# First stage of a hybrid block: attention units of one query block for two heads, with scores of 64 rows in row halves of TensorE

## The reference

```
x = X                                             # 16 x 512 tokens x 256
x = x + attn_a(layernorm(x))                      # 16 heads of 64, exact GELU on the heads, inner residual
x = x + ffn(layernorm(x))                         # ternary weights 256 -> 1024 -> 256, relu
x = x + attn_b(layernorm(x))                      # 16 heads of 16, rope, biases
x = x + ffn(layernorm(x))                         # the same ffn again
attn_a(X):  Q, K, V = X@Wq, X@Wk, X@Wv            # 256 -> 1024 each
            A = softmax(Q (K/8)^T) V ;  P = gelu(A) @ Wpost ;  return X + P
ffn(x):     Wq = clip(round(W / (mean|W| + 1e-5)), -1, 1) ;  relu(x@Wq1^T + b1) @ Wq2^T + b2
```

## Time and profile before

| | us |
|---|---|
| median of three runs | 4102.15 (4093.28 to 4102.24) |
| the profiled execution | 4105.4 |
| its span, first to last instruction | 4103.6 |
| PE, DVE, ACT, POOL busy | 3809.1, 2602.2, 2378.6, 1928.0 |
| first and last start of a score matmul of the first stage | 29.1, 2330.4 |

### The profile page before, as it was taken

How to read it: one execution, slowest core, us unless ns; L and a number is a source line. 1 busy time by engine, 2 the same in 40 slices (tenths; PEclk the granted TensorE clock), 3 DMA queues, 4 the chain that set the end, 5 groups by cost and what they waited for, 6 DMA issues and landing times.

```text
span 4103.6 us, 65459 instructions
## 1 busy us (share of the span) xinstructions
PE 3809.1 (93%) x23682; PEld 2700.6 (66%) x23682; DVE 2602.2 (63%) x4147; ACT 2378.6 (58%) x4593; POOL 1928.0 (47%) x1219
## 2 busy tenths in 40 slices
PE   7999999999999999999999878999999999999987
PEld 5777777777777777777777654555555555555544
DVE  5666666566566666656666756666666666666662
ACT  4655655556565555656556435666666666666654
POOL 3454555445455554545545444444444444444412
PEclk9999999999999999999999979999999999999998
DMA  4443443434434433443443423222222222222220
GB/s 128 93 103 88 93 101 92 97 91 98 101 84 97 103 89 92 103 94 87 103 98 83 112 53 52 53 53 53 53 53 53 53 53 53 53 53 53 48 43 16
DMA packets 152368, 315.59 MB, mean 77 GB/s; under 512 B 23088, under 2 KB 76720, under 8 KB 152048
## 3 DMA queue, kind: packets, MB, share of 16 engines
q1 hardware_dynamic: 152048, 311.39, 35.3%
HBM read 33.43 MB, written 25.17 MB: 14 GB/s over the span
## 4 chain that ended last, share of the span: by engine, by line
PE 56%; DVE 21%; ACT 13%; issue 7%; POOL 3%; SPq 1%; DMA 0%; DVEq 0%; POOLq 0%; ACTq 0%
PE ps_o L624 10%; DVE neg_max L970 7%; ACT e_a L788 6%; PE ps_o L701 5%; PE ps_t L216 5%; DVE max_b L1111 4%; PE ps_t L737 4%; PE ps_s L674 3%; ACT raw_a L812 3%; PE ps_t L660 3%; PE ps_t L223 3%; PE ps_t L728 3%; PE ps_t L608 3%; PE ps_m L216 2%; DVE xn L1089 2%
## 5 line engine op out<-in xcount | busy, mean ns | idle before, releaser
L497 POOL TENSOR_TENSOR e_a<-e_a,recip 128x1024 f32<-128x1024 f32 x512 | 969.5, 1893 | 1050.2 <-DVE recip L977 1050.2
L788 ACT ACTIVATE e_a<-ps_s,neg_max 128x512 f32<-128x512 f32 x1024 | 694.0, 684 | 245.4 <-DVE neg_max L970 234.2
L828 ACT ACTIVATE et<-ps_s 128x1024 f32<-128x1024 f32 x512 | 523.5, 1023 | 434.9 <-PE ps_s L688 434.9
L1111 DVE TENSOR_REDUCE max_b<-ps_s 128x2 f32<-128x1024 f32 x512 | 623.8, 1219 | 210.4 <-PE ps_s L674 209.1
L970 DVE TENSOR_REDUCE neg_max<-ps_s 128x2 f32<-128x1024 f32 x512 | 621.0, 1213 | 19.2 <-PE ps_s L596 19.2
L624 PE MATMUL ps_o<-et_a,v_a 128*64 128x256 f32 x4096 | 470.3, 382 | 0.0
L608 PE MATMUL ps_t<-ident,e_a 128*128 128x128 f32 x2736 | 394.6, 275 | 42.0 <-DVE et_a L984 35.8
L595 PE MATMUL ps_s<-stack_a 128*128 128x512 f32 x1024 | 412.5, 403 | 9.2 <-ACT e_a L788 7.7
L531 POOL TENSOR_TENSOR h_lo<-h,h_hi 128x512 fp32r<-128x512 f32 x256 | 329.3, 1302 | 180.9 <-ACT h_hi L872 180.9
L596 PE MATMUL ps_s<-stack_a 128*128 128x512 f32 x1024 | 402.1, 393 | 0.0
L608 PEld LDWEIGHTS ps_t<-ident,e_a 128*128 128x128 f32 x2736 | 321.1, 141 | 110.8 <-DVE et_a L984 51.9
(11 more groups left out here) (207 smaller groups left out, 7976.9 us busy)
## 6 DMA issues: line engine op xcount, KB each, us to landing
stack_a<-raw_a SPq DMA_DIRECT2D x256, 384.0 KB, 4.7
stack_a<-raw_a SPq DMA_DIRECT2D x256, 256.0 KB, 4.3
stack_a<-raw_a SPq DMA_DIRECT2D x256, 128.0 KB, 3.5
q_stack<-roped_q SPq DMA_DIRECT2D x256, 64.0 KB
k_stack<-roped_k SPq DMA_DIRECT2D x256, 64.0 KB
x_a<-X SPq DMA_DIRECT2D x16, 512.0 KB, 3.6
X<-x_a SPq DMA_DIRECT2D x16, 512.0 KB, 2.9
x_ahead<-X SPq DMA_DIRECT2D x16, 512.0 KB, 3.9
```

Of the source, the lines that this page charges most:

```text
L497: nc.gpsimd.tensor_tensor(e_a[:, u % 4, :, :], e_a[:, u % 4, :, :], factor, ALU.mult).then_inc(e_normed, 1)
L788: ins = nc.scalar.activation(e_a[:, u % 4, j, :], ps_s[:, 2 * (u % 2) + j, :], ACT.Exp, bias=neg_max[:, u % 4, j:j + 1], accum_out=sums[:, ...
L828: nc.scalar.activation(et[:, v % 5, :, :], ps_s[:, 2:4, :], ACT.Exp)\
L1111: nc.vector.reduce_max(max_b[:, u // 4 % 2, :, u % 4], ps_s[:, score_bank(u):score_bank(u) + 2, :], AX.X, negate=True).then_inc(max_done, 1)
```

## The change

A unit becomes one query block for both heads of a pair; four units are still a pair. The six DMAs a pair and `stack_a` are gone. The scores of a head are three matmuls of 64 rows, directly from `raw_a`: head 0 from rows 0 to 63, head 1 from rows 64 to 127, alternating, into different banks. One call makes two units, in even slots only, 12 matmuls, and it waits for the exponentials of every earlier unit. The lead of the scores over the transposes is four slots in place of three; exponentials have five buffers in place of four. The values of a pair are made in two halves, each of 8 products, in odd slots, ahead of the slot's transposes. The table is laid out so that nearly every slot has one product; the output projection fills a bank for each of four token blocks, in place of two blocks a fill. In slots 4 and 20 of a batch element, VectorE copies both fills of the transposes. W1 and W2 are loaded in slot 40, their sums are taken in slots 471 and 473, and quantising is in slots 504 and 506. At the start, ScalarE makes the high parts of four of the six weight pieces.

```diff
-        XT, QK_FIRST, VALUE_SLOTS = -10, -8, ((-6, -5, -2, -1), (3, 3, 7, 15))
-        POST = ((27, 31), (42, 43))
+        XT, QK_SLOTS = -9, (-7, -6)
+        FIRST_VALUES, VALUE_SLOTS = (-5, -4, -1, 0), ((-8, -5, -4, -1), (7, 8, 15, 16))
+        POST, LAST_POSTS = ((32, 32, 35, 36), (43, 44, 51, 52)), (45, 46, 47, 48)
...
+        GELUS, BOTH_TURNED = (19, 35), (4, 20)
+        LEAD = 4
+        LOAD_W, LOAD_WB, LOAD_REST, SPLIT, ABS = 40, 484, 503, (508, 509), (471, 473)
+        GAMMA, QUANTISE, SCALE, CLEAR = 474, (504, 506), 514, (513, 514)
...
-                    for h in range(2):
-                        src = slice(HA * h, HA * (h + 1))
-                        dst = stack_a[:, n % 2, h, :, :].bitcast(F32)
-                        sp.dma_start(dst[0:HA, 0, :], raw[src, 0, :]).then_inc(stacked[n % 2], 16)
-                        sp.dma_start(dst[0:HA, 1:3, :], raw[src, 2:4, :]).then_inc(stacked[n % 2], 16)
-                        sp.dma_start(dst[HA:P, :, :], raw[src, 1:4, :]).then_inc(stacked[n % 2], 16)
...
                 def a_scores(u):
-                    if u >= 2:
-                        pe.wait_ge(a_exp_done, u - 1)
-                    st = stack_a[:, n % 2, h, :, :]
+                    if u:
+                        pe.wait_ge(a_exp_done, u)
+                    raw = raw_a[:, n % 2, :, :]
                     for j in range(2):
-                        c = (2 * half + j) * P
-                        out = ps_s[:, 2 * (u % 2) + j, :]
-                        mm(out, st[:, 0, c:c + P], st[:, 1, :], start=True, stop=False)
-                        last = mm(out, st[:, 0, c:c + P], st[:, 2, :], start=False, stop=True)
-                    last.then_inc(a_qk_done, 1)
+                        c = (u % 4 + j) * P
+                        for m, (q_part, k_part) in enumerate(((0, 2), (0, 3), (1, 2))):
+                            for h in range(2):
+                                rows = slice(HA * h, HA * (h + 1))
+                                last = mm(ps_s[:, 2 * j + h, :], raw[rows, q_part, c:c + P], raw[rows, k_part, :],
+                                          start=(m == 0), stop=(m == 2))
+                        last.then_inc(a_qk_done, 1)
...
-                        if 0 <= slot + 3 < UNITS_ALL:
-                            a_scores(slot + 3)
+                        if slot % 2 == 0 and 0 <= slot + LEAD < UNITS_ALL:
+                            a_scores(slot + LEAD)
+                        if slot % 2 == 1 and 3 <= slot < UNITS_ALL:
+                            a_values((slot - 3) // 2)
...
-                        if 0 <= slot < UNITS_ALL:
+                        if 0 <= slot < UNITS_ALL and slot % UNITS not in BOTH_TURNED:
                             a_copy_turned(slot)
-                        if 0 <= slot + 3 < UNITS_ALL:
-                            a_exps(slot + 3)
+                        if 0 <= slot + LEAD < UNITS_ALL:
+                            a_exps(slot + LEAD)
```

More of the change, by code:

```diff
@@ L370, in a_load_x @@
                 def a_load_x(s):
-                    if s >= 2:
-                        sp.wait_ge(a_x_out, 16 * (s - 1))
+                    sp.wait_ge(a_stats_ready, 2 * s)
+                    if s >= 3:
+                        sp.wait_ge(a_x_out, 16 * (s - 2))
                     sp.dma_start(xa_of(s), X[s, :, :].rearrange("(t p) d -> p t d", p=P)).then_inc(a_x_in, 16)
                 def a_save_x(s):
-                    for two in range(2):
-                        wait_emptied(sp, fill_of["post", 1, two, s])
+                    for tok in range(TB):
+                        wait_emptied(sp, fill_of["post", 1, tok, s])
@@ L654, in a_product @@
                         pe.wait_ge(parts_ready, PAIRS * s + 4 * a + 4)
-                        for t in (2 * b, 2 * b + 1):
-                            for k in range(4):
-                                p = 4 * a + k
-                                parts = parts_of(PAIRS * s + p)
-                                for m, (part, w) in enumerate(((0, wpost_hi), (0, wpost_lo), (1, wpost_hi))):
-                                    last = mm(bank(fill)[:, (t % 2) * D:(t % 2 + 1) * D], parts[:, part, t * P:(t + 1) * P],
-                                              w[:, p, :], start=(k == 0 and m == 0), stop=(k == 3 and m == 2))
+                        for k in range(4):
+                            p = 4 * a + k
+                            parts = parts_of(PAIRS * s + p)
+                            for m, (part, w) in enumerate(((0, wpost_hi), (0, wpost_lo), (1, wpost_hi))):
+                                last = mm(bank(fill)[:, 0:D], parts[:, part, b * P:(b + 1) * P], w[:, p, :],
+                                          start=(k == 0 and m == 0), stop=(k == 3 and m == 2))
                     last.then_inc(bank_filled[fill % 3], 1)
@@ L974, in a_invert @@
                     dve.wait_ge(a_exp_done, u + 1)
-                    if u >= 4:
-                        dve.wait_ge(e_normed, u - 3)
-                    nc.vector.reciprocal(recip[:, u % 4, :], sums[:, u % 4, :]).then_inc(recip_ready, 1)
+                    if u >= 5:
+                        dve.wait_ge(e_normed, u - 4)
+                    nc.vector.reciprocal(recip[:, u % 5, :], sums[:, u % 5, :]).then_inc(recip_ready, 1)
                 def a_copy_turned(u):
-                    fill = fill_of["turn", 0, u]
-                    wait_filled(dve, fill)
-                    if u >= 5:
-                        dve.wait_ge(a_values_done, (u - 5) // 4 + 1)
-                    emptied(nc.vector.tensor_copy(et_a[:, u % 5, 0:2, :].rearrange("p t s -> p (t s)"), bank(fill)), fill)
+                    for part in range(2 if u % UNITS in BOTH_TURNED else 1):
+                        fill = fill_of["turn", part, u]
+                        wait_filled(dve, fill)
+                        out = et_a[:, u % 4, 2 * part:2 * part + 2, :, :].rearrange("p t h q -> p (t h q)")
+                        emptied(nc.vector.tensor_copy(out, bank(fill)), fill)
                 def a_low(todo):
@@ L1005, in a_low @@
                         dve.wait_ge(res_ready, s + 1)
[L1006 to L1007 removed]
+                        x = xa_of(s)[:, b, :]
+                        emptied(nc.vector.tensor_tensor(x, x, bank(fill)[:, 0:D], ALU.add), fill)
                 def a_copy_values(n):
[L1010 removed]
+                    dve.wait_ge(a_values_done, 2 * n + 2)
                     if n >= 6:
```

196 lines of the change are left out of this document (98 added, 98 removed).

## The result

| | median us | ratio to the kernel before | 95% interval |
|---|---|---|---|
| before (4 runs beside it) | 4100.4 | | |
| changed kernel (4 runs) | 4136.5 | 1.0092 | 1.0076 to 1.0108 |

The change costs 36 us, 0.9%, and the interval lies wholly above 1. I had forecast 4097 us and no measurable change. (The ratio is worked out from all the runs and not from the two medians, so it differs from their quotient in the last digit.) The profiled execution after has a span of 4138.2 us, 34.6 more than before.

The account below looks back on a forecast made before the run. TensorE was taken as the bound, with 8.82 us loops and extras making 144.5 us a batch element against 144.1. Then 4105.4 + 6 - 3 - 8 = 4100 us profiled, forecast 4097; range 4005 to 4190, the forecast's own 4075 to 4120.

Parts of the forecast that it names:

- What bounds the kernel before: First stage: TensorE bounds it, 144.1 us a batch element, of which 130.4 is work and some 13.7 gaps.
- The score visit: TensorE's two-unit score matmuls: 1.60 us, 0.24 less than before, with row-half pairs side by side and 0.11 at each end.
- The wait that is tightened: Even-slot scores wait for the previous slot's exponentials, behind ScalarE's copy: TensorE stands 0.79 us, while most bank waits go.
- The loop: Two slots of the first stage, from TensorE's transposes through ScalarE back to scores: 2.61 plus 6.21, 8.82 us.
- My own sign: If the first stage ends before 2270 us or after 2340, the loop is wrong and not the ends.
- Extras: Additions for a batch element: 1.4 us for two output products in slot 0, 2.0 us behind the GELUs.
- The GELU lag: Behind each set of GELUs, VectorE's reciprocal waits for late exponentials, delaying the next maximum: 1.0 us, twice a batch element.
- Ends of the stage: First stage's start, waiting for value weights: -3 us; its end, with quantising on VectorE earlier: -8 us.
- VectorE closes the loop: Slower rival: odd-slot maximum comes late on VectorE, exponentials behind it; 0.3 us a loop, 77 us, 4175 us; chance 0.21.
- Hidden ends: Faster rival: TensorE's waits hide loads and mode switches; loop 8.53 us, about 4000 us, half gives 4045; chance 0.32.
- loads in the open: Slower rival: every score pair shows its weight load, 2.04 us a visit, +113 us, 4210 us; chance 0.04.
- halves one after the other: Slower rival: the two row halves run in sequence in score visits, +1.38 us each, 353 us, 4450 us; chance 0.03.

Follow-up runs that it names:

- exponentials and maximum first: Changed kernel with, in odd slots, ScalarE's exponentials ahead of its copy and VectorE's maximum ahead of reciprocal and low part: 3955.8 us, 0.9652 of the kernel before.
- one-row-half run: Changed kernel with the scores of both heads made from rows 0 to 63, so all 12 matmuls use one half: 4509.8 us, one run.
- the one swap: Changed kernel with ScalarE making exponentials ahead of its copy of the transposes in odd slots: 4031.9 us, 0.9834 of the kernel before.
- the last experiment: Kernel with both orders swapped (3955.8 us), its value halves moved to even slots right behind the score visit: 4145.0 us, 1.0115 of the kernel before.
- maximum first alone: Changed kernel with only VectorE's maximum ahead of reciprocal and low part in odd slots, ScalarE's order unchanged: 4124.5 us, 1.0063 of the kernel before.
- weights-late run: Changed kernel with W1 and W2 loaded in slot 500, summed in 503 and 506, quantised in 509 and 510: 4136.0 us, 1.0092 of the kernel before.
- second swap: VectorE's maximum ahead of reciprocal and low part in odd slots, added to the changed kernel with ScalarE's exponentials first: 3955.8 us, 0.9652 of the kernel before.

## Why the prediction was wrong

**What bounds the kernel before.** Right, but its base was off. My 144.1 us was a mean over the whole stage. The first batch element is only 138.9 long, the steady ones 144.95. Against the true base my 144.5 would have been a gain of 0.4 us a batch element, and not a loss of 0.4; the miss of the loop is the 2.4 us between 144.5 and 146.94. Part of the 13.7 us that I called gaps is work, too: a product behind transposes takes 1.48 us and not 1.39 (below).

**The score visit: right.** Forecast 1.60 us, measured 1.59 (1007.25 to 1008.84). Where the visit waits for nothing, another 0.10 stands ahead of it: in the kernel with exponentials and maximum first, the product there takes 1.58 us (1000.65 to 1002.23) and not the 1.47 that it takes ahead of transposes. The rule of the Trainium skill, "TensorE: Matmul & The Clock Gate", Part 3, that weight loads overlap with matmuls in flight only when the row group differs, would have given the 2.04 of my estimate; the trace excludes it here. The same part's statement that matmuls on different tiles of the array run concurrently is borne out by the one-row-half run, 1.66 us on two halves against 3.01 on one.

**The wait that is tightened: right in place and size, and this is where the expected gain went.** Forecast: about 0.79 us in every second slot, and bank waits gone. Measured: 0.61 to 0.93 us before each visit, 0.70 on average (152.2 us in 218 waits), and hardly a bank wait. Taking it away by the one swap gave 105 us, and putting it into the old kernel cost 214, a part of them by the clock.

**The loop: the step that failed.** The step "The loop is 8.82 us for two slots" measured 9.05: its terms were each the right ones, and some were too small. The steady loss comes from it. By its terms, against the timeline above, which is one of the loops of 9.09:

| term | forecast | measured |
|---|---|---|
| even slot's product, to the values | 1.39 | 1.57 |
| half the values, to the transposes | 1.91 | 1.88 |
| first transposes and copy on ScalarE | 0.44 + 0.63 | 1.13 |
| copy to exponential, two exponentials | 0.49 + 1.44 | 0.49 + 1.44 |
| hand-over to TensorE | 0.05 | 0.15 |
| score visit, eight transposes (mean of the two slots) | 1.60 + 0.87 | 1.59 + 0.85 |
| sum | 8.82 | 9.10 |

The product is the term most in error, by 0.18 us. My 1.39 was read where a product follows the output projection. One that follows transposes took 1.48 in the kernel before as well:

```profile
604.79 0.48 PE L216 MATMUL ps_t<-xh_a,wa_hi 128*128 128x512 f32 x1
...
606.27 0.39 PE L595 MATMUL ps_s<-stack_a 128*128 128x512 f32 x1
```

The other 0.09 stands between the product and the values, on column halves; ahead of transposes a product takes 1.47 in the changed order too, as the last experiment shows. Leaving the column halves makes the transposes and the copy 0.06 longer. The half of the values itself is 0.03 shorter than I had it, so the entry of 0.11 that I gave it was in the wrong place, and product with values took 3.45 us against 3.30. The hand-over was 0.10 us longer than the one case I had read it from. Each is a tenth of a microsecond, but there are 256 loops: 0.23 x 256 = 59 us. The forecast range held them, the forecast itself did not. My own sign had been that a stage which ends after 2340 us means a wrong loop; the last score visit starts at 2359.7.

**Extras.** Two products in slot 0: forecast 1.4, measured 10.49 - 9.09 = 1.40. The GELU lag: forecast 1.0 us each, measured 0.28 (9.33 against 9.05). That it comes through VectorE's order was right, since maximum first alone takes it away; its size was not. So 16 x 9.05 + 1.4 + 0.6 = 146.8, close to the measured 146.94. Of the 59 us, the smaller lag gives back 1.4 x 16 = 23.

**Ends of the stage.** The start was right: the first transposes stand at 37.24 in place of 41.01, -3.8 us for a forecast of -3. The end was wrong: forecast -8. From those transposes to the first matmul of the feed-forward layer (L728) it is 2355.5 us against 2316.7, 38.8 more, of which 16 x 1.99 = 32 are loops. Of the other 7, 1.5 lie in the first batch element, and the rest, with 3 more until the second stage's attention units begin, is the end; the rest of the second stage then gives 3 back. The weights-late run shows that the early weights, from which I had taken my 8 us, neither won nor lost anything. In the last two score visits the scores wait 2.33 and 4.03 us, and behind these waits the granted clock is 0.50, the lower level: the visits are busy for 2.59 and 2.93 us in place of 1.66:

```profile
2348.57 2.59 PE L594 MATMUL ps_s<-raw_a 64*128 64x512 f32 x12 [2.33 <-ACT e_a L790]
```
```profile
2349.20:2352.20 3.00, 3.00 (x15) 2.28 (x12) 1.23 (x1) 0.00 (x0) 3.00 (x3) 0.50 0.38 107
2359.50:2362.50 3.00, 2.77 (x12) 1.83 (x12) 1.24 (x2) 0.18 (x2) 2.39 (x2) 0.50 0.00 0
```

The kernel before has a stretch at 0.50 there too, so how much of the end this explains stays open.

**Where the 40 us went.** Against a forecast of -5 us, the span of the profiled execution grew by 34.6. The loops and their extras make 26 of the difference (32 in place of 6: 39 too little for the changed kernel, less the 14 by which my base was too low), the end 14 (6 in place of -8), the start -1.

**Rivals.** "VectorE closes the loop" gave the right sign by the wrong mechanism: maximum first alone changed only the GELU lag. Hidden ends, loads in the open, and halves one after the other are all excluded by the timeline. I had written 0.34 for slower. The mistake in the chances, as I read it now, was to treat the terms of the loop as if errors of a tenth could go both ways: a boundary that I had not seen could only add.

## What to carry to other kernels

When a wait is moved one slot closer, look at what stands ahead of the awaited instruction on its own in-order engine; here one copy ahead of the exponentials tied them to the waiter's own latest work, and swapping two calls turned +0.9% into -1.7%, with a second swap -3.5%. Add such a loop up from starts, not from durations, and read each term where it has the same neighbours as in the new order, because a tenth of a microsecond returns hundreds of times. After one bound goes, read the waits again: the second swap was worth 12 us before the first and 76 after it.

## What the runs showed of the hardware

Matmuls of 64 rows on the two row halves ran side by side although three of one half stood in a row before three of the other: 12 of them in a visit of the same length (1.66 us busy), in loops of 9.00 to 9.10 us. All 12 on one half were busy for 3.01 in place of 1.66 us. Both are single runs. Going from row halves straight to column halves left the score visit at 1.59 us and saved one change of shape elsewhere, 0.16 us a loop: 0.10 in the product that no longer stands ahead of values, and 0.06 in the transposes that no longer stand behind them. In the old kernel with the tightened wait, the granted clock fell to 0.50, the lower of its two levels, after a wait of 3.01 us, while the changed kernel, with waits of up to 0.93 us, stayed at 1.00 from 200 to 2200 us.
